# k and v of a last layer's attention projected ahead from context columns, and half the score products, in a four-layer kernel

## The reference, cut to what matters

```python
h  = rmsnorm(x, ln1_w);  kv = rmsnorm(ctx, ln1_w)     # v * rsqrt(mean(v^2) + 1e-6) * ln1_w
q = (h @ Wq)             # 16 heads of 64
k = (kv @ Wk)            # 4 heads of 64, each serves 4 heads of q
v = (kv @ Wv)
q = q * cos + rotate_half(q) * sin      # rotate_half(x) = concat(-x2, x1)
k = k * cos + rotate_half(k) * sin
probs = softmax(q @ k.T / 8 + mask)
hidden = x + (probs @ v) @ Wo
out = hidden + (silu(n @ Wgate) * (n @ Wup)) @ Wdown  # n = rmsnorm(hidden, ln2_w)
```

## Time and profile before

| | us |
|---|---|
| median of three runs (511.89 to 514.20) | 512.62 |
| profiled execution | 513.77 |
| span of its trace | 512.0 |

### The profile page before, as it was taken

The page is one execution under the profiler, slowest core; times in us unless marked ns, Lnnn a source line. Parts: engine busy times, 40 slices in busy tenths (PEclk is TensorE's granted clock), DMA queues, the critical chain, the costliest instruction groups (busy, mean ns, idle before and its releaser), DMA issues.

```text
span 512.0 us, 17286 instructions
## 1 busy us (share of the span) xinstructions
PE 463.3 (91%) x7032; PEld 377.1 (74%) x7032; DVE 353.5 (69%) x893; ACT 306.5 (60%) x738; POOL 271.3 (53%) x331
## 2 busy tenths in 40 slices
PE   4899999999999999897767778999999999999885
PEld 4577778777787877786655567888888888878674
DVE  6778756577677777475767645869687786767542
ACT  1377777677777777757443636574656555555441
POOL 5475876679787788634343523545443445451210
PEclk9799999999999999999979988999999999999999
DMA  8950000000000000000000000000000000000000
GB/s 293 234 197 3 3 2 3 3 3 3 3 1 3 4 3 3 1 1 2 1 0 3 1 3 1 3 13 1 13 2 13 3 1 13 3 12 1 13 2 20
DMA packets 12277, 11.36 MB, mean 22 GB/s; under 512 B 5160, under 2 KB 10152, under 8 KB 12200
## 3 DMA queue, kind: packets, MB, share of 16 engines
q1 hardware_dynamic: 11624, 9.01, 6.4%
q10 hardware_dynamic: 576, 1.26, 0.7%
HBM read 9.22 MB, written 1.05 MB: 20 GB/s over the span
## 4 chain that ended last, share of the span: by engine, by line
PE 63%; issue 12%; DVE 9%; POOL 8%; ACT 6%; DMA 1%; POOLq 0%; DVEq 0%; ACTq 0%
PE ps L468 7%; PE ps L642 5%; PE ps L482 4%; PE ps L756 4%; PE ps L658 4%; PE ps L458 4%; PE ps L680 4%; PE ps L450 4%; PE ps L637 3%; PE ps L650 2%; PE ps L408 2%; PE ps L688 2%; PE ps L779 2%; PE ps L493 2%; PE ps L409 2%
## 5 line engine op out<-in xcount | busy, mean ns | idle before, releaser
L1256 DVE TENSOR_REDUCE negm<-ps 128x8 bf16<-128x512 f32 x96 | 59.6, 683 | 26.0 <-PE ps L450 26.0
L856 ACT ACTIVATE shared<-ps 128x512 f32<-128x512 f32 x96 | 57.2, 601 | 20.9 <-PE ps L468 19.1
L1643 POOL TENSOR_TENSOR rstd<-veps,neghalf 128x2 f32<-128x2 f32 x40 | 28.9, 723 | 74.1 <-DVE veps L1280 55.4
L1716 POOL TENSOR_TENSOR wide<-wide,cv 128x1024 f32<-128x1024 f32 x24 | 45.4, 1893 | 30.6 <-DVE wide L1235 30.6
L468 PE MATMUL ps<-cst,p 128*128 128x128 f32 x384 | 58.7, 276 | 0.4 <-ACT shared L856 0.4
L468 PEld LDWEIGHTS ps<-cst,p 128*128 128x128 f32 x384 | 45.2, 141 | 16.1 <-issue 9.5
L850 ACT ACTIVATE p<-ps 128x512 f32<-128x512 f32 x96 | 54.3, 596 | 4.1 <-PE ps L458 4.0
L1766 POOL TENSOR_TENSOR probs<-p,rc 128x512 f32<-128x512 f32 x32 | 33.0, 1044 | 35.1 <-DVE rc L1524 35.0
L1041 ACT ACTIVATE late<-ps 128x512 f32<-128x512 f32 x32 | 17.3, 592 | 34.1 <-PE ps L779 34.1
L658 PE MATMUL ps<-wo,late 128*128 128x128 f32 x256 | 32.7, 282 | 2.5 <-ACT late L1041 2.5
L658 PEld LDWEIGHTS ps<-wo,late 128*128 128x128 f32 x256 | 31.7, 197 | 4.1 <-issue 3.5
(11 more groups left out here) (199 smaller groups left out, 1193.2 us busy)
## 6 DMA issues: line engine op xcount, KB each, us to landing
late<-in_mask_l SPq DMA_DIRECT2D x2, 512.0 KB, 12.3
result<-x_all SPq DMA_DIRECT2D x8, 128.0 KB, 1.8
x_all<-in_x_tok SPq DMA_DIRECT2D x1, 768.0 KB, 7.4
wide<-in_ctx_t SPq DMA_DIRECT2D x1, 768.0 KB, 8.9
rv<-in_rv ACTq DMA_DIRECT2D x1, 768.0 KB, 8.1
wa<-in_wa SPq DMA_DIRECT2D x1, 512.0 KB, 10.8
w<-in_w SPq DMA_DIRECT2D x2, 256.0 KB, 7.8
wq<-in_wq SPq DMA_DIRECT2D x1, 512.0 KB, 7.5
```

Of the source, the lines that this page charges most:

```text
L856: A_(pt[:, w % 2, r, :], ring_of("p", w, r), ACT.Copy).then_inc(sm["act_pt"], 1)
L1256: V.tensor_reduce(negm[:, n % 4, :], ps[:, S_BANK[r], :].rearrange("p (a k) -> p a k", k=S), AX.X, ALU.max, negate=True).then_inc(sm["dve_ ...
L1716: P.tensor_tensor(r_op[:, w % 2, :, :], k_t[:, w % 2, :].unsqueeze(1).to_broadcast([128, 4, GT]), head_masks.unsqueeze(2).to_broadcast([12 ...
```

## The change

Five things are done together. First, k and v are projected from the columns of the raw context (ctx_t), which stay in SBUF; Wk and Wv are scaled by ln1_w once on ACT, and the factor rsqrt(mean square) of each context token is applied when ACT reads k and v out of PSUM. The 16 squares of the context are taken during the attention. Only x is normed in the rounds, so "in" is two transposes and not four. Second, k and v are made three rounds ahead and kt two (KEPT = 4 copies). Third, the 64 positions of a head are permuted so that the partner of each in the rotation lies 16 partitions away: a shuffle within 32 partitions swaps them. DVE reads q by a shuffle (PSUM to the buffer qsh) and a product with cos, and POOL multiplies qsh by sin and adds it to q (turn_q; q1 and q3 of group 0 on DVE, turn_own). The score products are one set, 64 a half and not 128, and ks is gone. Fourth, k is copied by ACT to SBUF (kk), rotated by DVE from there (rotate_k) and summed by POOL in one addition. Fifth, fills are moved: nearly all of RAMP into the FFN, and the orders of all four lists are rewritten around that.

```diff
+PARTNERS = np.arange(HD3).reshape(2, 2, 16).transpose(1, 0, 2).reshape(HD3)
+EXCHANGE = [p ^ 16 for p in range(32)]
+KEPT = 4
...
         HALVES = (
             (("s0", 0), ("s1", 0), ("pv0", -1), ("pv1", -1), ("l_in", 2), ("md", -2), ("l_text", 2), ("out", -1),
-             ("l_gate", 2), ("t0", 0), ("in", 1), ("t1", 0), ("k", 1), ("q0", 1), ("q1", 1)),
-            (("s0", 0), ("s1", 0), ("pv0", -1), ("pv1", -1), ("m_in", -1), ("kt", 1), ("ks", 1), ("q2", 1), ("q3", 1),
-             ("out", -1), ("v", 1), ("mg0", -1), ("mu0", -1), ("l_back", 2), ("t0", 0), ("mg1", -1), ("mu1", -1), ("t1", 0)),
+             ("in", 1), ("l_gate", 2), ("t0", 0), ("q0", 1), ("t1", 0), ("q1", 1), ("kt", 2)),
+            (("s0", 0), ("s1", 0), ("pv0", -1), ("pv1", -1), ("q2", 1), ("m_in", -1), ("q3", 1), ("k", 3), ("out", -1),
+             ("mg0", -1), ("mu0", -1), ("v", 3), ("l_back", 2), ("t0", 0), ("mg1", -1), ("mu1", -1), ("t1", 0)),
         )
         OPENING = (
-            (("s0", 0), ("s1", 0), ("l_back", 1), ("l_in", 2), ("l_text", 2), ("l_gate", 2), ("t0", 0), ("t1", 0)),
-            (("s0", 0), ("s1", 0), ("pv0", -1), ("pv1", -1), ("in", 1), ("out", -1), ("k", 1), ("q0", 1), ("q1", 1),
-             ("l_back", 2), ("kt", 1), ("ks", 1), ("q2", 1), ("q3", 1), ("v", 1), ("t0", 0), ("t1", 0)),
+            (("s0", 0), ("s1", 0), ("kt", 1), ("k", 2), ("l_gate", 2), ("t0", 0), ("in", 1), ("t1", 0), ("q0", 1), ("q1", 1)),
+            (("s0", 0), ("s1", 0), ("pv0", -1), ("pv1", -1), ("q2", 1), ("q3", 1), ("kt", 2), ("k", 3), ("out", -1),
+             ("v", 3), ("l_back", 2), ("t0", 0), ("t1", 0)),
         )
         ENDING = (
             (("pv0", -1), ("pv1", -1), ("out", -1), ("md", -2)),
@@ -259,13 +268,15 @@
         )
         ROUNDS = range(NG + 2)
 
-        EARLY_A = {3: ("l_text", 0), 4: ("l_in", 1), 5: ("l_gate", 1)}
-        EARLY_B = {2: ("l_in", 0), 3: ("l_gate", 0), 4: ("l_text", 1), 5: ("l_back", 0)}
-        EARLY = [part[g] for g in range(NG + 1) for part in (EARLY_A, EARLY_B) if g in part]
-        RAMP = (("in", 0), ("k", 0), ("q0", 0), ("q1", 0), ("kt", 0), ("ks", 0), ("q2", 0), ("q3", 0), ("v", 0))
+        EARLY_A = {2: (("k", 0),), 3: (("l_text", 0),), 4: (("v", 0),), 5: (("kt", 0),), 6: (("l_gate", 1),),
+                   7: (("v", 1),), 8: (("q0", 0), ("q1", 0))}
+        EARLY_B = {2: (("l_in", 0),), 3: (("l_gate", 0),), 4: (("l_in", 1),), 5: (("l_text", 1), ("l_back", 0)),
+                   6: (("k", 1),), 7: (("in", 0),)}
+        EARLY = [use for g in range(NG + 1) for part in (EARLY_A, EARLY_B) for use in part.get(g, ())]
+        RAMP = (("q2", 0), ("q3", 0), ("l_in", 2), ("l_text", 2), ("v", 2), ("l_back", 1))
         PER_UNIT = {"s0": "s3x", "s1": "s3x", "t0": "t3e", "t1": "t3e", "pv0": "pv3e", "pv1": "pv3e"}
...
             def part_q(g, i):
+                if i == 0:
+                    pe.wait_ge(*released("in", g))
                 for j in range(2):
-                    ins = mm(bank_of(f"q{i}", g)[:, j * GT:j * GT + GT], wq3[:, 2 * i + j, :], hn_t[:, g % 2, 0:GT],
+                    ins = mm(bank_of(f"q{i}", g)[:, j * GT:j * GT + GT], wq3[:, 2 * i + j, :], hn_t[:, g % 2, :],
                              start=True, stop=True, skip_group_check=True)
                 return ins
 
             def part_kv(what, g):
-                if what == "k":
-                    pe.wait_ge(*released("in", g))
+                pe.wait_ge(sm["w_ln"], 2)
                 for i in range(TG):
...
-                                    for j in range(2):
-                                        rows = slice(j * S, j * S + S)
-                                        ins = mm(banks[j][h * S:h * S + S, cols], q3[gs][a][rows, c, 2 * i + h, toks[b]],
-                                                 k3[rows, gs, c, a, toks[b]], start=False, stop=True, skip_group_check=True)
+                    if u == 0:
+                        if a == 0:
+                            pe.wait_ge(*released("kt", g))
+                        pe.wait_ge(sm["q_rot"], turned(g, 2 * a + 1))
+                        if own_turn(g, 2 * a + 1):
+                            pe.wait_ge(sm["q_own"], 2 * a + 2)
+                    for i in range(2):
+                        for b in range(2):
+                            cols = slice(((2 * a + i) * 2 + b) * S, ((2 * a + i) * 2 + b) * S + S)
+                            for h in range(2):
+                                for j in range(2):
+                                    rows = slice(j * S, j * S + S)
+                                    ins = mm(banks[j][h * S:h * S + S, cols], q3[gs][rows, a, 2 * i + h, toks[b]],
+                                             k3[rows, g % KEPT, a, toks[b]], start=False, stop=True, skip_group_check=True)
                 ins.then_inc(sm["s3"], 1)
...
-                    ins = A_(v3[:, gs, :, :].rearrange("p t n -> p (t n)"), bank, ACT.Copy)
+                    act.wait_ge(sm["c_r"], 1)
+                    if what == "k" and g >= 1:
+                        act.wait_ge(sm["d_kc"], g)
+                    if what == "v" and g >= KEPT:
+                        act.wait_ge(sm["pv3"], TG * (g - KEPT + 1))
+                    dst = kk if what == "k" else v3[:, g % KEPT, :, :]
+                    for t in range(TG):
+                        n = TG * g + t
+                        ins = A_(dst[:, t, :], bank[:, t * NK3:t * NK3 + NK3], ACT.Copy, scale=rsc[:, n:n + 1])
                 ins.then_inc(sm["a_use"], 1)
...
-                kcv = kc[:, :, :].rearrange("p t (n d) -> p (t n) d", d=HD3)
-                ksv = ks[:, :, :].rearrange("p t (n d) -> p (t n) d", d=HD3)
+                if n >= 2:
+                    if own_turn(*divmod(n - 2, 4)):
+                        dve.wait_ge(sm["q_own"], n - 1)
+                    else:
+                        dve.wait_ge(sm["q_rot"], turned(*divmod(n - 2, 4)))
+                bank = bank_of(f"q{i}", g)
+                V.stream_shuffle(qsh[:, n % 2, :], bank, EXCHANGE)
+                return V.tensor_tensor(q_rows(g, i), bank.rearrange("p (b q) -> p b q", q=S), q_table(0), ALU.mult)
+
+            def turn_own(g, i):
+                n = 4 * g + i
+                dve.wait_ge(*released(f"q{i}", g))
+                V.tensor_tensor(q_swapped(g, i), q_swapped(g, i), q_table(1), ALU.mult).then_inc(sm["q_own"], 1)
+                dve.wait_ge(sm["q_own"], n)
+                V.tensor_tensor(q_rows(g, i), q_rows(g, i), q_swapped(g, i), ALU.add).then_inc(sm["q_own"], 1)
+
+            def rotate_k(g):
+                dve.wait_ge(*released("k", g))
+                if g >= 1:
+                    dve.wait_ge(sm["d_kr"], g)
+                    dve.wait_ge(sm["p_use"], filled("kt", g - 1))
+                k = kk.rearrange("p t (n h s d) -> p (t n) h s d", h=2, s=2, d=16)
+                own = ks.rearrange("p t (n h s d) -> p (t n) h s d", h=2, s=2, d=16)
+                tab = cst[:, C_SIN:C_SIN + HD3].rearrange("p (h s d) -> p h s d", h=2, s=2)
                 n = TG * NKV
-                V.tensor_tensor(kcv, k, cst[:, C_COS:C_COS + HD3].unsqueeze(1).to_broadcast([128, n, HD3]), ALU.mult)
+                V.tensor_tensor(kc[:, :, :].rearrange("p t (n d) -> p (t n) d", d=HD3), kk.rearrange("p t (n d) -> p (t n) d", d=HD3),
+                                cst[:, C_COS:C_COS + HD3].unsqueeze(1).to_broadcast([128, n, HD3]), ALU.mult)
                 for j in range(2):
-                    tab = cst[:, C_SIN + j * half:C_SIN + j * half + half].unsqueeze(1).to_broadcast([128, n, half])
-                    ins = V.tensor_tensor(ksv[:, :, j * half:j * half + half], k[:, :, (1 - j) * half:(2 - j) * half], tab,
-                                          ALU.mult)
-                return ins
+                    ins = V.tensor_tensor(own[:, :, :, j, :], k[:, :, :, 1 - j, :],
+                                          tab[:, :, j, :].unsqueeze(1).to_broadcast([128, n, 2, 16]), ALU.mult)
+                ins.then_inc(sm["d_kc"], 1)
...
             def second_half(r):
                 n = 2 * r + 1
                 live = r < NG
-                if r + 1 < NG:
-                    read("q0", r + 1)
-                    read("q1", r + 1)
                 if live:
                     smax3(2 * n)
                     smax3(2 * n + 1)
+                if r + 1 < NG:
+                    read("q2", r + 1)
                 if r + 2 < NG:
                     l2_weigh(r + 2)
-                if live:
-                    sum3(2 * n)
-                if r + 1 < NG:
-                    read("q2", r + 1)
-                if live:
-                    sum3(2 * n + 1)
                 if r + 1 < NG:
                     read("q3", r + 1)
                 if live:
+                    sum3(2 * n)
+                    sum3(2 * n + 1)
                     read("out", n - 1)
                 if 0 <= r - 1 < NG:
                     read("mg0", r - 1)
                     read("mu0", r - 1)
+                if r + 3 < NG:
```

(84 more changed lines are left out.)

241 lines of the change are left out of this document (133 added, 108 removed).

## The result

The changed kernel takes 534.47 us (median of 4 runs, 532.98 to 535.19), the kernel before 513.41 on the same chip: ratio 1.039, 95% interval 1.0355 to 1.0425. It is 21 us slower; the prediction had the sign, and a quarter of the size. The profiled execution took 534.9 us, its span 533.1.

A forecast was written before the change was run, and what follows sets the result against it. PE bound the steady round before; after, POOL's row and DVE's waits for POOL would. Rounds 1 to 5 +4.2, round 6 -2.7, end -2.0, start +6.0, attentions +0.4: +5.9 on 513.77, 519.7, taken as 518 us, range 502 to 526.

The forecast's parts named there:

- The rotation of k waits for POOL: First half of a steady round: rotate_k's three products grow from 1.44 to about 4 us, the half from 14.23 to 15.4.
- POOL's unbroken row: Second half of a steady round: POOL's turns, logits, fuse and probs hold t0 until T1+10.85; half 14.2 where 13.83.
- POOL pays nothing: Steady rounds: probs beside DVE work with two SBUF inputs take 1.04 on average, none much longer; only DVE waits.
- rival 1: Steady rounds: POOL has slack, the round falls to PE's work, 24.7 to 26.3; whole 491 to 504 us; chance 0.17.
- rounds 1 to 5, +4.2: Five rounds at 29.4 us each, 147.0 where they took 142.84: +4.2, bounds -2.3 and +5.7.
- at about T1+1.6: Second half of a round: DVE has read q1 about 1.6 us after T1, the half's first score.
- From there POOL does not stop: Second half: from q1's read POOL runs unbroken through turns, logits and fuse to the first probs, at T1+10.8.
- the start, +15.4 against +6.4: Up to round 1: first scores +9.5, opening round -3.5, net +6.0 (bounds 0 and +9), and +0.4 in the attentions.
- The last mlp_down [...] ends at about 264.5: End of the FFN: its last product, 254.88 to 258.06 before, ends at about 264.5 after PE's waits.
- The opening round loses what it had to do then: Opening round: with in, k, kt, ks and other fills gone it takes 27.5 for 31.00 us, -3.5.
- The end, -0.7 against -2.0: Round 7 and what is behind it: two score blocks of 1.0 us each go, -2.0.
- The gain on PE: Steady round: scores, ks, in and the wait for hn_t save 3.4 us; 28.06 becomes 24.7 if nothing else is late.

The follow-up runs named there:

- e2: Changed kernel with rotate_k reading k of groups 2 and up from PSUM, ACT's copies and the context's norm factor left out: 526.40 us, ratio 1.026.
- e3: Changed kernel with the product by sin left out of every turn of q on POOL: 518.73 us, ratio 1.010 to the kernel before.
- e11: Kernel before with k and v from raw context (norm factors left out) and the score products against q times sin left out: 496.42 us, ratio 0.968.
- e4: Changed kernel with wvis of group 0 and its fusion product on POOL placed sooner in the FFN: 530.37 us, ratio 1.033 to the kernel before.
- e5: Changed kernel with wvis of group 0 sooner and the last mlp_down ahead of in, q0 and q1 on PE: 525.67 us, ratio 1.027.
- e8: Changed kernel with wvis and the last mlp_down sooner, and k of groups 2 and up scaled and rotated from PSUM: 516.35 us, ratio 1.008.

## Why the prediction was right and wrong

The forecast's sum was +5.9, the spans differ by 21.1. Of the 15.2 between them 9.0 lie at the start, 5.0 in rounds 1 to 5 and 1.3 at the end.

**Right: what would bind the round.** Behind PE the forecast named two mechanisms, and each was found. The rotation of k waits for POOL: three products of 3.66 us (4 forecast), statistics at 379.82, 0.75 into round 3 (1 forecast), t0 at 390.18, 11.1 into it (11.5), first half 15.00 (15.4). POOL's unbroken row: POOL is busy 22.1 a round (22.2), t0 of the second half at 405.50, 11.43 behind T1 (10.85), half 14.91 (14.2). e2 and e3 show both as causes and not only as company, though e3 shortens the rotation's wait as well. By the Trainium skill (SBUF — State Buffer, Who interferes with whom) a DVE instruction with two SBUF inputs and a GpSimd instruction that reads SBUF exclude each other, and the later one waits; the trace agrees for both engines: DVE's pair took 2.90 for 0.74, and POOL's turn 1.73 for 1.26. The forecast had read in the rows of before that POOL pays nothing. By rival 1 the round would have fallen to PE's work, 24.7; e11, with nothing added but ks still in, is at 25.5.

**Mis-sized: rounds 1 to 5, +4.2 against +9.2.** Rounds 2 and 3 took 29.9 where 29.4 was taken, 0.5 each. The term that was short is that DVE has read q1 "at about T1+1.6", and "From there POOL does not stop": in round 3 POOL is still in the turn of q0 then, and q1's starts at 396.32, 2.2 behind T1 (394.07). Rounds 4 and 5 took 30.6 with the same work: their first halves are 15.66 and 15.67 at a clock of 0.89, where rounds 2 and 3 have 15.0 at 1.00. Round 1 was taken at 29.4 too and was 30.98, its first half 16.08 at 0.89. It was no steady round before either: 30.54, its first half 16.71 at 0.90. To take it at 29.4 was to forecast a gain there that no term gave. Together: 0.5 in each of rounds 2 to 5 is 2.0, the two halves at the lower clock 1.3, and round 1 1.6, which is 4.9 of the 5.0 that the forecast lacked.

**Wrong: the start, +15.4 against +6.4 (the attentions with it).** The step that failed is "The last mlp_down [...] ends at about 264.5": it ended at 269.0, which is 4.5 of the 9.0. The list of POOL and DVE had been walked, PE's order at the FFN's end had not: EARLY_A[8] puts q0 and q1 ahead of mlp_down(7). e4 and e5 give 7.9 us back with that and wvis. What stands behind it took 17.8 to the first score, 16.8 forecast. Second, "The opening round loses what it had to do then", 27.5 for 31.00: it took 31.36, another 3.9. That term had counted PE's work, though the prediction itself reads PE busy 23.60 of 31.00 there and leaves the opening to the chain through the other engines. In it in(1) needs the norm of group 1, whose l_back now comes just ahead of the first score; in stands at 298.43, 11.6 into the round, DVE reads q from 301.83, and POOL's turns begin at 303.2. What was moved out of the opening shortened nothing there, and the products of its first half run at a clock of 0.60. This reading is from the chain of the changed kernel alone; no run moved l_back(1). POOL has a part in it, since e3 has the opening at 29.07.

**The end, -0.7 against -2.0.** The two score blocks are gone. In the changed kernel the last 30.25 us ran at a clock of 0.94, before 29.99 at 0.99; e3 and e8, where the clock stayed up, have 37.7 for round 7 and the end, 2.1 less than before, as forecast.

**The gain on PE.** It was there: e11's 17 to 18 us, without ks. The change spends them on POOL (e3: 16 us for half of its turns), on a second SBUF input (e2: 8) and on where the first groups stand (e5: 9). The first two overlap and are no sum.

## What to carry to other kernels

When an engine binds with 98% of a round, look for the chain that stands next to it before its work is counted as gain: here it stood 1 us behind, and two savings gave 2.5 together and 1.0 alone. Before a DVE product is given a second SBUF input, look at what POOL does at that time. When fills are moved ahead into a stage that is in order, walk every engine's list, the bound one's first: what stands behind a moved fill waits for its inputs too.

## What the runs showed of the hardware

A DVE operation on four numbers waited as well: L1465 of the changed kernel, TENSOR_SCALAR with one SBUF input and a result in SBUF, takes 746 ns on average, L1398 of the kernel before, the same operation away from POOL's work, 170. The eight of L1465 go from 0.17 to 1.04; the one at 391.46 takes 0.89 and ends when POOL's addition does (391.05, 1.28).

```profile
L1465 DVE TENSOR_SCALAR agm<-agm 128x4 f32<-128x4 f32 x8 | 6.0, 746 | 0.3
```

```profile
L1398 DVE TENSOR_SCALAR agm<-agm 128x4 f32<-128x4 f32 x8 | 1.4, 170 | 0.3
```

So "one SBUF input" is no safe rule; the products that read PSUM were. The shuffle, which no row of before had, took 732 ns from PSUM, near any pass over 512 elements.

PE's idle time cost again afterwards: after the wait of 5.03 us the granted clock of the next 3.23 us is 0.58, and 1.00 for the same eight products 7 us later (first the stretch and its us, then PE, PEld, DVE, ACT, POOL, clock):

```profile
247.10:250.33 3.23, 3.23 (x12) 2.64 (x11) 0.00 (x0) 1.23 (x3) 0.00 (x0) 0.58 0.02 5
254.36:256.25 1.89, 1.89 (x10) 1.68 (x9) 1.81 (x12) 0.84 (x2) 1.64 (x3) 1.00 0.00 0
```

That is between the two levels of 1.2 and 2.4 GHz, nearer the lower. The products of q0 and q1 behind the wait of 3.72 ran at 0.53 (263.70 to 267.06). In the rounds of the changed kernel the lower clock goes with the longer time, 29.9 at 1.00 and 30.6 with a first half at 0.89, where PE is busy 13.6 for 12.2. That PE's idle time in the rounds is the reason was not shown, and what decides when the clock falls in a round with the same waits as its neighbour was not settled.
